# An attention and routed-FFN block in fp32 accuracy: q and k as two fp32r parts in the two halves of the partitions, and the last projection tile rearranged

## The reference

```python
qkv = jnp.einsum('btc,oc->bto', x, w_attn)
q, k, v = jnp.split(qkv, 3, axis=-1)          # 32 heads of 16
q, k = _apply_rope(q, cos, sin), _apply_rope(k, cos, sin)
scores = jnp.einsum('bhqd,bhkd->bhqk', q, k) / jnp.sqrt(hd)
scores = jnp.where(causal, scores, -jnp.inf)
y = jnp.einsum('bhqk,bhkd->bhqd', jax.nn.softmax(scores, axis=-1), v)
y = y + softmax(q @ ak / sqrt(C)) @ av * gating
x = _layernorm(x + y @ w_proj.T)
x = _layernorm(x + ffn(x))                    # base_w, base_b, router_w, A, B
```

## Time and profile before

| | us |
|---|---|
| median of 3 runs | 995.81 |
| the profiled execution | 998.74 |
| its span (first to last instruction) | 996.8 |
| PE busy | 904.7 (91%) |
| DVE busy | 742.4 (74%) |
| ACT busy | 488.3 (49%) |
| POOL busy | 234.0 (23%) |
| mean granted TensorE clock | 0.951 of 2.4 GHz |

### The profile page before, as it was taken

One profiled execution on the slowest core, in us unless ns is written; L12 is line 12 of the kernel. 1 busy time (PEld: TensorE's weight loads), 2 busy tenths in 40 slices (PEclk: granted clock), 3 DMA queues, 4 the chain that ended last, 5 costly groups with the idle time before them and its releaser, 6 DMA issues. The chain is left out here.

```text
span 996.8 us, 16045 instructions
## 1 busy us (share of the span) xinstructions
PE 904.7 (91%) x5420; PEld 504.6 (51%) x5420; DVE 742.4 (74%) x2253; ACT 488.3 (49%) x1026; POOL 234.0 (23%) x251
## 2 busy tenths in 40 slices
PE   6899999776999999999999999999848999999996
PEld 4678787462222232222222322222237888888884
DVE  5474766578698988889898889896156677777766
ACT  3243434212577777777777777777841221221210
POOL 0324243204122222222122222222202122122211
PEclk9899999886599999999999999999968999999998
DMA  6124242225553334554334445325110010110110
GB/s 238 32 70 114 71 117 68 80 64 124 101 97 67 64 65 95 97 96 86 64 61 81 96 97 96 77 61 156 46 42 11 22 43 21 42 42 21 43 32 32
DMA packets 50410, 73.11 MB, mean 73 GB/s; under 512 B 8996, under 2 KB 21540, under 8 KB 50340
## 3 DMA queue, kind: packets, MB, share of 16 engines
q1 hardware_dynamic: 50340, 72.22, 31.6%
HBM read 55.12 MB, written 16.78 MB: 72 GB/s over the span
## 5 line engine op out<-in xcount | busy, mean ns | idle before, releaser
L744 ACT ACTIVATE pt<-bank 128x512 f32<-128x512 f32 (+3 forms) x768 | 335.1, 493 | 112.1 <-PE bank L1251 101.8
L907 DVE CUSTOM_DVE_ANT_0 bank<-bank,cmask 128x512 f32<-128x512 f32 (+3 forms) x512 | 234.8, 524 | 22.1 <-PE bank L1261 20.2
L1251 PE MATMUL bank<-qs,ks 98*128 98x512 bf16 (+3 forms) x768 | 212.1, 339 | 23.5 <-ACT pt L744 23.4
L910 DVE TENSOR_REDUCE mx<-bank 128x1 f32<-128x512 f32 x256 | 159.5, 686 | 11.3 <-PE bank L1261 9.0
L1349 PE MATMUL bank<-pt,vb 128*32 128x512 f32 (+3 forms) x1536 | 166.9, 507 | 0.9 <-POOL pt L592 0.9
L592 POOL TENSOR_SCALAR_AFFINE_SELECT pt<-pt 128x512 f32<-128x512 f32 x128 | 81.2, 634 | 366.3 <-ACT pt L744 366.3
L1261 PE MATMUL bank<-km,qm 48*128 48x512 bf16 (+3 forms) x768 | 132.0, 343 | 16.8 <-DMA km<-k_parts 5.9
L1251 PEld LDWEIGHTS bank<-qs,ks 98*128 98x128 bf16 x768 | 59.8, 97 | 162.6 <-ACT pt L744 99.4
L1261 PEld LDWEIGHTS bank<-km,qm 48*128 48x128 bf16 x768 | 33.7, 94 | 141.8 <-DVE mx L907 58.7
L769 ACT CAST xth<-bank 128x512 fp32r<-128x512 f32 x16 | 9.4, 586 | 153.4 <-PE bank L1413 153.4
L907 DVE DVE_READ_ACCUMULATOR2_ANT mx<- 128x1 f32 x512 | 73.1, 143 | 0.0
(11 more groups left out here) (143 smaller groups left out, 1377.6 us busy)
## 6 DMA issues: line engine op xcount, KB each, us to landing
qs<-q_parts SPq DMA_DIRECT2D x32, 256.0 KB
q_parts<-part SPq DMA_DIRECT2D x48, 128.0 KB, 2.4
k_parts<-part SPq DMA_DIRECT2D x48, 128.0 KB, 2.4
ks<-k_parts SPq DMA_DIRECT2D x16, 384.0 KB
qm<-q_parts SPq DMA_DIRECT2D x32, 128.0 KB, 7.7
km<-k_parts SPq DMA_DIRECT2D x32, 128.0 KB, 7.2
qs<-q_parts SPq DMA_DIRECT2D x32, 128.0 KB
ks<-k_parts SPq DMA_DIRECT2D x16, 256.0 KB
```

The costliest lines, as they stand in the source:

```text
L744: act.activation(pt[k % PT_BUFS][:, h, 0:width(st)], half(n % SCORE_BUFS)[:, 0:width(st)], ACT.Exp, scale=float(HD) ** -0.5).then_inc(S("e ...
L907: last = ve.tensor_tensor_reduce(blk, blk, cmask[:, BANK - nk * P:], 1.0, NEG, ALU.add, ALU.max, mx[m][:, 0, h, qt:qt + 1])
L910: last = ve.tensor_reduce(mx[m][:, 1, h, qt:qt + 1], blk, AX.X, ALU.max)
L1251: pe.matmul(half(n % SCORE_BUFS)[:, 0:q1 - q0], ks[g % 2][0:KX, h, kb * P:(kb + 1) * P], qs[g % 2][0:KX, h, q0:q1], start=True, stop=True) ...
```

## The change

It has three parts.

1. **Parts of q and k.** Two fp32r parts in place of three bf16 ones, in DRAM as fp32. ACT makes one copy a unit, POOL one subtraction, SP stores with 4 transfers of 256 KB in place of 6 of 128 KB. `remainders`, `second` and the tile `rem` go.
2. **One set of tiles.** `qm` and `km` go, `qs` and `ks` take their layout: 3 products (`TERMS`, 48 rows) and two rows for the maximum, heads in the two halves of the partitions (0 to 49, 64 to 113), three buffers. Maxima and scores both read them, so `load_max` and `load_scores` become `load_group`, 8 transfers a group. The matmuls of both kinds are fp32r; the score matmuls of heads 0 and 2 use the lower half of the rows, those of 1 and 3 the upper. `store_max` has two transfers in place of one, `load_ones` six in place of two.
3. **Order.** In projection tile 0 the four adapter transposes (line 1169) stand after the second v block and no longer before the first. In each tile ACT evacuates banks 8 and 9 ahead of `first(tau, 2)`. The loads of group 0 are issued by ACT at the end of the third tile. In the last tile PE makes max tiles 16 to 25 among unit 3 and none ahead of it, and 26 to 35 after; DVE takes tiles 16 to 35, joins and copies the maxima, and only then rotates unit 3. SP loads group 1 after the last v and y blocks. POOL builds v for group 0 before its last subtraction.

```diff
-PARTS = 3
-TERMS = [(0, 0), (0, 1), (0, 2), (1, 0), (1, 1), (2, 0)]
+PARTS = 2
+TERMS = [(0, 0), (1, 0), (0, 1)]
 KR = len(TERMS) * HD
 KX = KR + 2
+HALF = P // 2
...
-EARLY = (16, 28)
+EARLY = (16, 26)
...
-            for i in range(2):
-                qm[i] = sb(b, f"qm{i}", [P, 2, T], BF16)
-                km[i] = sb(b, f"km{i}", [P, 2, T], BF16)
-            for i in range(2):
-                qs[i] = sb(b, f"qs{i}", [P, HG, T], BF16)
-                ks[i] = sb(b, f"ks{i}", [P, HG, T], BF16)
+            qs, ks = [None] * 3, [None] * 3
+            for i in range(3):
+                qs[i] = sb(b, f"qs{i}", [P, 2, T], F32R)
+                ks[i] = sb(b, f"ks{i}", [P, 2, T], F32R)
...
+        def issue_group(eng, g):
+            for dst, src, pick in ((qs[g % 3], q_parts, 0), (ks[g % 3], k_parts, 1)):
+                heads = src[g * HG:(g + 1) * HG].rearrange("(r a) s d t -> a s d r t", a=2)
+                for r, n, p0 in runs(pick):
+                    for par in range(2):
+                        r0 = HALF * par + HD * r
+                        eng.dma_start(dst[r0:r0 + HD * n].bitcast(F32),
+                                      heads[par, p0:p0 + n].rearrange("s d r t -> (s d) r t")).then_inc(S(f"qk{g % 3}"), 16)
...
+            def load_group(g):
+                if g >= 3:
+                    sp.wait_ge(S("score_full"), SCORE_BANKS * (g - 2))
+                issue_group(sp, g)
...
-                    else:
-                        load_first()
...
-                    else:
-                        load_max(1)
                     store_unit(b, u, tau, 2)
                     if not more:
                         sp.wait_ge(S("value_full"), NV * TILES)
-                        load_scores(0)
+                        load_group(1)
...
             def sp_group(g):
-                if g + 1 < G:
-                    load_scores(g + 1)
                 if g + 2 < G:
-                    load_max(g + 2)
+                    load_group(g + 2)
...
+            def remainder(tau, j):
+                gp.wait_ge(S("part_high"), 4 * tau + j + 1)
+                gp.tensor_tensor(part[j % 2][:, 1], rope[j % 2][:], part[j % 2][:, 0], ALU.subtract).then_inc(S("part_low"), 1)
...
+                    evac(tau, 8, pat[0][:], vb_(8)[0:80].rearrange("p (g n) -> p g n", g=4))
+                    evac(tau, 9, pat[1][:], vb_(9)[0:80].rearrange("p (g n) -> p g n", g=4))
                     first(tau, 2)
                     if tau + 1 < TILES:
                         x_high(tau + 1, 1 - u, 1)
...
+                    if tau == TILES - 2:
+                        for n in range(2):
+                            act.wait_ge(S(f"pst{n}"), HEAD[f"pst{n}"] + 16 * 4 * NTT * 2)
+                        issue_group(act, 0)
...
-                        for w in range(EARLY[0], EARLY[1]):
+                        for w in range(EARLY[0], NMX):
                             max_bank(0, w, w)
+                        max_rows(0, NMX)
+                        copy_rows(0, NMX)
                     rotate(tau, u, 3)
...
-                pe.matmul(half(n % SCORE_BUFS)[:, 0:q1 - q0], ks[g % 2][0:KX, h, kb * P:(kb + 1) * P],
-                          qs[g % 2][0:KX, h, q0:q1], start=True, stop=True).then_inc(S("score_full"), 1)
+                r0 = HALF * (h % 2)
+                pe.matmul(half(n % SCORE_BUFS)[:, 0:q1 - q0], ks[g % 3][r0:r0 + KX, h // 2, kb * P:(kb + 1) * P],
+                          qs[g % 3][r0:r0 + KX, h // 2, q0:q1], start=True, stop=True).then_inc(S("score_full"), 1)
...
-                    last = pe.matmul(out[:, col:col + nk * P], qm[g % 2][r0:r0 + KM, pr, qt * P:(qt + 1) * P],
-                                     km[g % 2][r0:r0 + KM, pr, k0 * P:(k0 + nk) * P], start=True, stop=True)
+                    last = pe.matmul(out[:, col:col + nk * P], qs[g % 3][r0:r0 + KR, pr, qt * P:(qt + 1) * P],
+                                     ks[g % 3][r0:r0 + KR, pr, k0 * P:(k0 + nk) * P], start=True, stop=True)
...
                         values(tau, u, a_, first_part)
                         first_part()
+                        if tau == 0 and a_ == 1:
+                            adapter_transposes()
...
                     a_trans(tau, 0, 4)
                     a_trans(tau, 1, 5)
-                    second_part()
                     unit_half(tau, u, 3, 0, second_part)
```

More of the change, by code:

```diff
@@ L174, in norm_use, with runs @@
     return use_of(g + 1, NORM_AT[0]) if g + 1 < G else USE0[G]
[L177 to L181, removed]
 NTC = NB * QT
-EARLY = (16, 28)
+EARLY = (16, 26)
 CW = [("w_projT", 0), ("base_wT", 0), ("B_T", 0), ("B_T", CC)]
[L193 to L198, removed]
+def runs(pick):
     out, r = [], 0
-    while r < len(terms):
+    while r < len(TERMS):
         n = 1
-        while r + n < len(terms) and terms[r + n][pick] == terms[r + n - 1][pick] + 1:
+        while r + n < len(TERMS) and TERMS[r + n][pick] == TERMS[r + n - 1][pick] + 1:
             n += 1
-        out.append((r, n, terms[r][pick]))
+        out.append((r, n, TERMS[r][pick]))
         r += n
     return out
-SCORE_LOADS = len(runs(TERMS, 0)) + len(runs(TERMS, 1))
-MAX_LOADS = 2 * (len(runs(MAX_TERMS, 0)) + len(runs(MAX_TERMS, 1)))
+LOADS = 2 * (len(runs(0)) + len(runs(1)))
 def drive_tiles(eng, step):
@@ L255, in build @@
             rope = [sb(a, f"rope{i}", [P, 2, TT]) for i in range(2)]
-            rem = sb(a, "rem", [P, 2, TT])
+            rtmp = [sb(a, f"rtmp{i}", [P, TT]) for i in range(2)]
             xh, xl = [None, None], [None, None]
@@ L263, in build @@
             xs = sb(a, "xs", [P, 2, TT])
-            rtmp = [sb(a, f"rtmp{i}", [P, TT]) for i in range(2)]
-            part = [sb(a, f"part{i}", [P, PARTS, 2, TT], BF16) for i in range(2)]
+            part = [sb(a, f"part{i}", [P, PARTS, 2, TT], F32R) for i in range(2)]
             pat = [sb(a, f"pat{i}", [80, 4, P]) for i in range(2)]
@@ L425, in store_unit @@
                         sp.dma_start(dst[:, r, 8 * hf:8 * hf + 8, u * TT:(u + 1) * TT],
[L426 to L436, removed]
-                            sp.dma_start(dst[r0:r0 + HD * n], heads[par, p0:p0 + n].rearrange("s d r t -> (s d) r t")
-                                         ).then_inc(S(f"qkmax{g % 2}"), 16)
@@ L585, in build_v @@
                                ).then_inc(S("v_built"), 1)
+            for tau in range(TILES):
+                for j in range(NU):
+                    if tau == TILES - 1 and j == NU - 1:
+                        gp.wait_ge(S("value_full"), NV * TILES)
+                        gp.wait_ge(S("value_read"), HEAD["value_read"] + NV * (TILES - 1))
+                        for i in range(3):
+                            gp.memset(vb[i][:, :, :, HD:HD + 1], 1.0).then_inc(S("v_set"), 1)
+                            gp.memset(vb[i][:, :, :, HD + 1:VW], 0.0).then_inc(S("v_set"), 1)
+                        build_v(0)
+                    remainder(tau, j)
+            gp.wait_ge(S("part_low"), HEAD["part_low"] + 4 * TILES)
             def gp_group(g):
@@ L699, in _ @@
                     evac(tau, 3, v_out(3), vb_(3).rearrange("p (g n) -> p g n", g=GB))
-                    second(tau, 1)
                     for a_ in range(4):
@@ L899, in max_bank @@
                 pr, par, pieces = max_of(w)
-                h = 2 * pr + par
+                h = 2 * par + pr
                 ve.wait_ge(S("max_full"), use + 1)
```

123 lines of the change are left out of this document (44 added, 79 removed).

## The result

| | before | after |
|---|---|---|
| median, us | 995.01 (4 runs, 993.18 to 997.93) | 1091.89 (4 runs, 1080.44 to 1102.42) |
| the profiled execution, us | 998.74 | 1085.02 |
| its span, us | 996.8 | 1083.3 |
| mean granted clock, of 2.4 GHz | 0.951 | 0.832 |

A forecast was written before the change was run, and what follows sets the result against it. PE was taken to bound the projections, PE and DVE together mid-attention, DVE a little more. Terms summed to -18 us: 998.74 to 980.7 on the profiled execution, 977.8 on the median; range 957 to 1006.

The forecast's parts named there:

- (1): Projection tile 0: adapter transposes behind two v blocks lose PE's wait and the low clock after it, -6.0 us.
- (2): Projection tile ends: copying banks 8 and 9 earlier only moves PE's wait to x_low; 0.16 us a tile, -0.5 us.
- (3): Projections: dropped ACT copies, POOL subtractions and stores lie beside PE's work, so 0 us.
- (8): Attention: fewer q and k bytes a group stay hidden, the second transfer of maxima comes ahead of need; 0 us.
- (4): End of third projection tile: ACT issues group 0's loads, landing at 178 us; less fp32r load cost, net -2 us.
- (5): Last projection tile: with max tiles inside unit 3, DVE waits less for PE; -3.5 us.
- My run: Last projection tile: the new order played through with the same durations; DVE would wait some 3.5 us less.
- (6): First attention group, at 1.2 GHz with PE the bound: PE time given back counts double, -2 us.
- (7): Later attention groups at full clock: DVE stays the bound, its 30 waits at divisions shorten 0.13 us each, -4 us.
- the ends of PE's work: Groups at full clock: change in PE's work per group, between -5.8 and +5.9 us, taken as -1.
- the third rival: Attention: 1.2 GHz lasts one or two groups beyond the first, 8 us each, 990 us; chance 0.08.

The follow-up runs named there:

- halves_bf16: The changed kernel with its parts, rows of the maximum and ones in bf16 in place of fp32r; 963.43 us, ratio 0.9647 to the kernel before.
- halves_bf16_slow: halves_bf16 with six useless DVE clears added to each group, PE's work untouched; 975.65 us.
- halves_bf16_rows34: halves_bf16 with one more product left out: scores over 34 rows in place of 50, maxima over 32 in place of 48; 1198.13 us.

## Why the prediction was wrong, step by step

The number behind a term's name is what the prediction gave it, in us; one behind "right" or "wrong" is what was measured.

(1) Adapter transposes, -6.0: right. They run at 34.37 us without a wait, and the matmuls behind them keep records of 0.39 us. A later row of the same tile (transposes of `pa`, 0.24 us behind ACT in both programs) comes at 56.66 us, before at 62.56, -5.9.

(2) Banks 8 and 9, -0.5: wrong, +2.0. The wait did move to x_low, but it is no shorter (1.78 us against 1.57). And behind the start of the third tile, where the clock stayed full before (records of 0.39 us from 116.31 us on), it now falls:

```profile
110.36 0.50 PE L339 MATMUL bank<-xh,wh 128*128 128x512 f32 x1 [1.78 <-DVE xl L784]
...
111.28 0.63 PE L339 MATMUL bank<-xh,wh 128*128 128x512 f32 x1
```

The second tile begins 6.1 us earlier than before, the third 5.6, the fourth only 3.9 (157.33 against 161.22). I had counted the wait that goes with the one that comes, and not that a gap in another place may meet the clock otherwise.

(3) Nothing for ACT and POOL: right. (8) Nothing for traffic: right; PE waited 0.7 us in all for the stored rows of the maxima.

(4) Group 0 by ACT, -2: right in kind, -3.2. The first max tile, at 171.43 us, no longer waits for loads at all (5.93 us before), where I had put their landing at 178; the later ones wait for DVE instead (1.22 us at 174.80). The adapter scores come at 191.38 in place of 198.46, -7.1 in all.

(5) The last tile, -3.5: wrong, -0.6. The max tiles inside unit 3 made PE wait for DVE (2.87 us), the clock fell there, and the short matmuls behind ran at 1.2 GHz, so that DVE waited 3.59 us, about as long as before:

```profile
209.85 1.55 PE L1223 MATMUL bank<-ks,qs 48*128 48x128 f32 x4 [2.87 <-DVE mx L866]
211.33 2.07 PE L1188 MATMUL bank<-avbd,pat 80*128 80x128 f32 x8
```

```profile
215.92 0.43 DVE L866 CUSTOM_DVE_ANT_0 bank<-bank,cmask 128x256 f32<-128x256 f32 x1 [3.59 <-PE bank L1223]
```

The eight matmuls of L1188 take 2.07 us here and 1.05 at 219.77, at full clock. My run had used one duration for each and no such wait. The first score was to come 12 us earlier and came 7.7.

(6) The first group, -2: +1.1 in the changed kernel, -1.6 with 64 rows (31.06 us from the first score to the second store, against 32.70). With 64 rows the term comes out near its size; its first score comes 1.4 us later, though, since the fill loads hold up the rows of the maxima.

(7) The groups at full clock, -4: a group at full clock is as short as forecast, but in the changed kernel most groups are not at full clock. With 64 rows the fourteen groups take 406.4 us, -3.9. The reason that I gave isn't what happened, so this hit is luck: the waits of DVE ahead of the divisions, which were to shorten, are 1.42 and 0.86 us, 2.3 a group against 2.2 before. Here the waits of DVE and PE in one group after:

```profile
DVE rden L923 <- PE bank L1294: 2.3, 2, 1.4
PE bank L1213 <- ACT pt L704: 1.3, 2, 0.6
```

The 0.3 us are not traced further. Two scores do run at once: two of 128 columns take 0.33 us together at 311.80, before 0.51. Of the ends of PE's work, -5.8 and +5.9, the measured -0.42 lies near my -1. Halves and fp32r pull against each other: halves_bf16 has PE at 24.57 us, -3.5 against before, and fp32r gives 3.05 of it back; a load is recorded with 185 ns on average, a bf16 one with 93 to 96, but no run shows how much of the 3.05 that is. The 11.6 us that the prediction works out beside (7) count 108 loads of 107 ns; a group has 96, of 185 ns each in the trace, and the measurement decides.

**The step that failed** is the premise of (7), "the groups at full clock", and with it the third rival, which had the mechanism but not its size: "The clock stays low longer", one more group, 8 us, chance 0.08. It cost 82 us in the fourteen groups (488.4 less the 406.4 of 64 rows). Two things led there. I took the clock of before as given for every group but the first, and saw danger only in gaps of PE ("The gaps of 0.67 us leave the clock at full, and longer ones I don't foresee"). And I had the warning in hand and priced it by one group: the earlier trace rows shows the first group at 0.59 with PE busy 28.22 of 28.87 us, so that waits ahead of it may explain how the clock fell, but not why it stayed low, and I wrote that "the new scores fill half the rows". Nothing on record said that such a state would end after one group more. The range should have held that case: the same row prices a group at 1.2 GHz at 8 us more, fifteen groups at 120.

The last stretch was in no term: from the last store of maxima to the output stage it is 33.54 us before, 47.96 after and still 43.54 with 64 rows. There scores and products run without max tiles between them, and with 64 rows the clock is still low:

```profile
680.84:724.38 43.54, 36.54 (x186) 13.47 (x183) 4.24 (x7) 26.77 (x58) 7.83 (x12) 0.73 0.15 50
```

These 10 us, with (2), (5) and the later first score, are why the kernel with 64 rows gives 993.6 and not 978. The rows of an instruction don't settle the clock of this stretch by themselves: halves_bf16 and halves_bf16_slow have the same instructions in it, and it takes 44.43 us at 0.62 in the one and 33.60 at 1.00 in the other.

The Trainium skill (TensorE: Matmul & The Clock Gate, "HAM oscillation") puts a clock that swings down to idle gaps of PE. In the projections the trace agrees: the clock is at 1.2 GHz behind the wait of 3.17 us. In the attention no run bears it out: at 0.50 for 240 us in halves_bf16_rows34 PE idles for 3% and waits 0.7 us at the longest, at 0.98 in halves_bf16 it idles for 12% of a group and waits 0.7 us at the longest too. There the measurement decides.

**Open:** why 50 rows hold the clock in bf16 and not in fp32r (the period isn't it; the longer weight loads could be, no run takes them apart), how rows and running at once combine, and why the clock changes between groups with the same instructions. From the first store of maxima to the second it is low, 0.50 to 0.79, in every run, with 98 rows too; waits of PE stand at the start of that stretch, but the clock stays low long behind them. An fp32r kernel that fills both halves at once with all products, without a filler, was not tried.

## What to carry to other kernels

Before a change that makes matmuls fill fewer rows or lets two run at once, price the case that the granted clock falls: two programs that differ in fourteen filled rows of each half (and the twelve loads that fill them) are 89 us apart here. If the clock falls while PE is busy, try a contraction widened with zeros; it adds no matmul, only loads at the start, which must not stand ahead of what PE needs next. A low stretch in the profile of before with PE busy was the warning here.

Of the versions run, the kernel before with the new order (order_bf16, 0.9884) keeps the three parts of q and k; two bf16 parts in halves are faster (0.9647, and 0.9631 with 64 rows, which the intervals don't tell apart), with 16 bits of q and k where the three parts of the kernel before hold 24 (8 a part). The changed kernel with 64 rows only comes back to the time of before (0.9966).

## What was not expected of the hardware

- With matmul number, columns and order the same, the granted clock over fourteen groups was 0.77 at 50 rows, 0.85 at 56 and 1.00 at 64 (fp32r); 0.53 at 34 and 0.98 at 50 (bf16, at 34 the max tiles narrower too). Rows of zeros count (989.2 us, clock 1.00).
- Groups with the same instructions ran at 1.00, 0.75, 0.58 and 0.86 in one execution (after).
- The clock stayed at 0.50 for 240 us on end with PE busy 233.35 us of them (halves_bf16_rows34).
- A fp32r weight load of 128 columns is recorded with 185 ns, a bf16 one with 96; in the changed kernel at mixed clock 235.
- fp32r matmuls of a score and of a max tile do run at once: both start at 309.37 us (after).

```profile
309.37 0.50 PE L1213 MATMUL bank<-qs,ks 50*128 50x512 f32 x1
309.37 0.73 PE L1223 MATMUL bank<-ks,qs 48*128 48x512 f32 x2
```
